# A macaron block with gated delta-rule attention on one core: beta in the decay exponent, T and softplus on the scalar engine, the output product on 32x32 tiles

## The reference

```
ffn(y):   xr, xk = mixes of y and of y one token earlier
          out = sigmoid(xr W_r) * ((relu(xk W_k)^2) W_v)
attn(y):  q, k, v = silu(conv4(y W))      q = q/|q| * 16^-0.5    k = k/|k|
          beta = sigmoid(y Wb)            g = -exp(A_log) * softplus(y Wa + dt_bias)
          per token and head:  S = S exp(g)
                               S = S + k outer ((v - k S) * beta)
                               o = q S
          out = (o * rsqrt(mean(o^2) + 1e-5) * norm_w * silu(y Wg)) Wo
x = x + 0.5 ffn(norm x);   x = x + attn(norm x);   x = x + 0.5 ffn(norm x)
```

## Time and profile before

| | before |
|---|---|
| runs | 1873.6, 1883.21, 1891.46 us |
| profiled execution, its own time | 1883.35 us |
| its span, first to last instruction | 1881.6 us |
| mean granted TensorE clock | 0.965 |
| busy: PE, PE weight loads, VectorE, ScalarE, GpSimd | 92%, 79%, 81%, 58%, 23% |
| MATMUL records on PE | 45,312 |

### The profile page before, as it was taken

One profiled execution on the slowest core, in us unless ns is written; L12 is line 12 of the kernel. 1 busy time (PEld: TensorE's weight loads), 2 busy tenths in 40 slices (PEclk: granted clock), 3 DMA queues, 4 the chain that ended last, 5 costly groups with the idle time before them and its releaser, 6 DMA issues.

```text
span 1881.6 us, 101829 instructions
## 1 busy us (share of the span) xinstructions
PE 1739.6 (92%) x45312; PEld 1486.7 (79%) x45312; DVE 1521.0 (81%) x4294; ACT 1089.1 (58%) x2002; POOL 438.4 (23%) x357
## 2 busy tenths in 40 slices
PE   5699999999999999999999999999999999999986
PEld 4587888787888788888888888888888878888775
DVE  4877889887888988888887888898788898887852
ACT  5556665555665565666565666555566555565533
POOL 0222221222221222222121222122222222222200
PEclk9889999999999999999999999999999999999877
DMA  3000000000000000000000000000000000000000
GB/s 113 2 3 4 15 14 4 15 14 15 15 15 9 9 15 15 15 15 15 3 15 14 15 15 15 9 9 14 15 15 15 9 9 9 9 9 10 9 9 13
DMA packets 21590, 26.50 MB, mean 14 GB/s; under 512 B 2209, under 2 KB 20769, under 8 KB 21153
## 3 DMA queue, kind: packets, MB, share of 16 engines
q1 hardware_dynamic: 21152, 19.99, 3.3%
HBM read 11.59 MB, written 8.39 MB: 11 GB/s over the span
## 4 chain that ended last, share of the span: by engine, by line
PE 53%; DVE 28%; issue 11%; ACT 1%; POOL 1%; DVEq 1%; ACTq 0%; POOLq 0%
PE ps L244 23%; PE ps L226 11%; PE ps L235 8%; DVE CV L1067 6%; DVE prod L1082 4%; DVE TZ L1083 3%; PE ps L219 2%; PE ps L400 2%; DVE T L1102 2%; PE ps L212 2%; DVE st L1035 2%; DVE XR L1056 1%; PE ps L357 1%; PE ps L461 1%; PE ps L372 1%
## 5 line engine op out<-in xcount | busy, mean ns | idle before, releaser
L1067 DVE SCALAR_TENSOR_TENSOR CV<-ps,cw,CV 128x256 f32<-128x256 f32 x576 | 250.8, 477 | 22.2 <-ACT CV L686 15.0
L244 PE MATMUL ps<-QE,S 64*64 64x16 f32 x4096 | 251.6, 209 | 2.0 <-ACT S L631 1.3
L244 PE MATMUL ps<-WP,V 64*64 64x16 f32 x4096 | 250.1, 208 | 0.0
L244 PEld LDWEIGHTS ps<-QE,S 64*64 64x64 f32 x4096 | 216.4, 138 | 35.0 <-issue 31.2
L244 PEld LDWEIGHTS ps<-WP,V 64*64 64x64 f32 x4096 | 217.4, 138 | 0.0
L244 PEld LDWEIGHTS ps<-WP,KD 64*64 64x64 f32 x4096 | 127.1, 137 | 36.5 <-DVE WP L1125 22.7
L1082 DVE TENSOR_TENSOR prod<-A,TZ 128x30 f32<-128x30 f32 (+7 forms) x480 | 139.0, 290 | 13.3
L967 POOL TENSOR_TENSOR OSQ<-OSQ,SQ 128x512 f32<-128x512 f32 x32 | 40.6, 1269 | 459.8 <-ACT OSQ L840 459.8
L244 PEld LDWEIGHTS ps<-SA,M 32*32 32x32 f32 x8192 | 91.0, 108 | 68.9 <-issue 34.3
L244 PE MATMUL ps<-SA,M 32*32 32x16 f32 x8192 | 117.9, 181 | 28.8 <-DVE SA L1096 18.4
L244 PE MATMUL ps<-KQI,K 64*64 64x48 f32 x4096 | 141.8, 221 | 1.4 <-DVE CV L1067 0.7
(11 more groups left out here) (152 smaller groups left out, 4055.4 us busy)
## 6 DMA issues: line engine op xcount, KB each, us to landing
X<-in_x SPq DMA_DIRECT2D x32, 256.0 KB, 2.9
out_x<-X SPq DMA_DIRECT2D x32, 256.0 KB, 2.3
KQI<-in_blocks SPq DMA_DIRECT2D x2, 256.0 KB, 4.2
w_r_ffn<-in_wT_r_ffn SPq DMA_DIRECT2D x1, 256.0 KB, 3.3
w_k_ffn<-in_wT_k_ffn SPq DMA_DIRECT2D x1, 256.0 KB, 3.5
w_v_ffn<-in_wT_v_ffn SPq DMA_DIRECT2D x1, 256.0 KB, 4.4
w_k<-in_wT_k SPq DMA_DIRECT2D x1, 256.0 KB, 4.3
w_q<-in_wT_q SPq DMA_DIRECT2D x1, 256.0 KB, 4.5
```

What stands on the lines that cost most here:

```text
L244: last = mm(ps[rows, o:o + n], stat[rows, pk].rearrange("p s c -> p (s c)"), mov[rows], **flags)
L1067: last = stt(d4[:, m], src, cw[:, i, m, tap:tap + 1], d4[:, m], ALU.mult, ALU.add)
```

## The change

It has five parts.

1. The output product on 32x32 tiles. S4 and V4 become S2 and V2 with 2 slots. Each pack now takes 4 + 4 matmuls on 4 tiles instead of 2 + 2 on 2 tiles; ScalarE fills each with 2 operations instead of 4. The product is cut into 8 segments instead of 4.
2. Beta in the decay exponent. Before, `beta_in` (4 matmuls of 128x128) added log(beta) to the decays and a second exponential gave EA; be and be2 scaled the output of `t_product`. Now GpSimd puts log(beta) on the diagonal of the step matrix ST (`beta_diag`, `stat1`), so that E has beta in it. `beta_in`, `exp_a`, `beta_log`, `b_diag` and `b_reduce` go.
3. T and softplus on ScalarE. `t_out0/1` move from VectorE (2 operations each) to ScalarE (3 each). ScalarE's softplus part has 5 small operations (L772 to L780, before 2); VectorE keeps 5, before 9.
4. Fewer, wider VectorE operations: KP and AT become one tile GK, M2 and QE one tile MQ, so a `gram` takes 3 operations instead of 4 and a `d_out` 1 instead of 2. MQ has two buffers.
5. Finer segments, another order on each engine and another table of PSUM banks. Solving is cut into 30 segments, each 1 operation; `conv` waits per tap instead of for all before it; `t_product` has 4 segments, `b_product` 4. `k_proj`, `q_proj` and `ffn1_r` run a step earlier, others move within the step.

The diff, cut to its core:

```
-        K4, KD4, V4, S4 = (sb(n, [P, PACKS, HT, C]) for n in ("K4", "KD4", "V4", "S4"))
+        K4, KD4 = (sb(n, [P, PACKS, HT, C]) for n in ("K4", "KD4"))
+        V2, S2 = (sb(n, [P, PACKS, 2, C]) for n in ("V2", "S2"))
...
-                for pk in range(h * PACKS // 4, (h + 1) * PACKS // 4):
+                for pk in range(h * PACKS // 8, (h + 1) * PACKS // 8):
                     o = PS["o"] * BANK + pk * C
-                    pairs(o, C, S4, pk, QE[g % 2][:, pk * C:(pk + 1) * C], start=True, stop=False)
-                    last = pairs(o, C, V4, pk, WP[g % 2][:, pk, U:], start=False, stop=True)
+                    pairs(o, C, S2, pk, MQ[g % 2][:, pk, U:], start=True, stop=False)
+                    last = pairs(o, C, V2, pk, WP[g % 2][:, pk, U:], start=False, stop=True)
...
-            def beta_in(g):
-                pe.wait_ge(s["lb"], g + 1)
-                pe.wait_ge(s["e"], g + 1)
-                for ub in range(M * B):
...
             def d_product0(g):
                 pe.wait_ge(s["wp"], 2 * g + 1)
                 pe.wait_ge(s["gram_used"], 4 * g + 4)
+                if g < GROUPS - 1:
+                    pe.wait_ge(s["cv"], 6 * g + 12)
+                    pe.wait_ge(s["tapv"], g + 2)
...
             def ffn1_r(g):
                 pe.wait_ge(s["xr1"], g + 1)
+                pe.wait_ge(s["relu1"], g + 1)
...
+            def t_out0(g):
+                act.wait_ge(s["t_ps"], 4 * g + 2)
...
+                for h in range(2):
+                    own.done(af(WP[g % 2][:, rows, h * C:(h + 1) * C], src[:, :, C:U], ACT.Copy, scale=slot[:, h:h + 1]))
+                nc.scalar.copy(WP[g % 2][:, rows, U:], src[:, :, 0:C]).then_inc(s["wp"], 1)
...
+            def beta_diag(g):
+                tt(packs(LD[:]), along(cz[:, BH:2 * BH]), over_packs(diag), ALU.mult).then_inc(s["ld"], 1)
...
-                own.done(tt(packs(QE[g % 2][:])[:, rows], packs(QP[:])[:, rows], src[:, :, U:], ALU.subtract))
-                tt(M2[:, rows].rearrange("p k s c -> p k (s c)"), GI2[:, rows], src[:, :, 0:U], ALU.subtract).then_inc(s["mt"], 1)
+                tt(MQ[g % 2][:, rows], GQ[:, rows], src, ALU.subtract).then_inc(s["mt"], 1)
```

More of the change, by code:

```diff
@@ new lines, in _ @@
+                on(ffn1_r, step)
+                on(turn3, step - 4)
+                on(o_product, step - 3, 4)
+                on(o_product, step - 3, 5)
+                on(ffn1_v, step)
+                on(k_squares, step - 1)
+                on(o_product, step - 3, 6)
+                on(o_product, step - 3, 7)
+                on(v_proj, step - 1)
+                on(t_product, step - 2, 0)
+                on(t_product, step - 2, 1)
+                on(decay_sums, step - 1)
+                on(ffn3_k, step - 4)
@@ new lines, in _ @@
+                on(t_product, step - 2, 2)
+                on(t_product, step - 2, 3)
+                on(o_squares, step - 3)
+                on(turn2, step)
+                on(d_product0, step - 2)
+                on(d_product1, step - 2)
+                on(d_product2, step - 2)
+                on(d_product3, step - 2)
+                on(b_product, step - 2, 0)
+                on(k_proj, step)
+                on(decay_steps, step - 1)
+                on(b_product, step - 2, 1)
+                on(q_proj, step)
@@ L618, in _ @@
+                on(b_product, step - 2, 2)
+                on(b_product, step - 2, 3)
+                on(ffn3_r, step - 4)
+                on(chain, step - 2, 0)
+                on(gram0, step - 1)
+                on(gram1, step - 1)
+                on(gram2, step - 1)
+                on(chain, step - 2, 1)
+                on(gram3, step - 1)
+                on(chain, step - 2, 2)
         @block.scalar
@@ L865, in rstd2 @@
                 root(1, s["rstd2"])
-            def soft_ln(g):
-                act.wait_ge(s["uz"], g + 1)
-                af(lu[:], uz[:], ACT.Ln).then_inc(s["lnu"], 1)
             def norm2(g):
@@ L927, in _ @@
+                on(tap_q, step - 1)
+                silu_set()
+                on(tanh3, step - 5)
+                on(xt1, step)
+                on(s_slots, step - 3)
+                ln_exp_set()
+                on(soft_exp, step - 1)
+                on(rstd3, step - 4)
+                silu_set()
+                on(silu_v, step - 2)
+                on(silu_k, step - 1)
+                on(relu1, step)
+                on(norm3, step - 4)
                 on(xt3, step - 4)
-                silu_set()
@@ L929, in _ @@
-                on(silu_k, step - 1)
-                on(tap_q, step - 1)
-                on(s_slots, step - 3)
+                on(silu_q, step - 1)
+                on(square_k, step - 1)
                 on(gate, step - 1)
-                on(relu3, step - 4)
-                on(relu1, step)
-                on(silu_q, step - 1)
-                on(tanh3, step - 4)
-                on(tap_v, step - 1)
+                on(tanh1, step)
+                ln_exp_set()
+                on(k_root, step - 1)
@@ L939, in _ @@
+                on(gates_wide, step - 1)
         @block.gpsimd
@@ new lines, in _ @@
+                on(gram1, step - 2)
+                on(chain, step - 3, 1)
+                on(gram2, step - 2)
+                on(gram3, step - 2)
+                on(chain, step - 3, 2)
+                on(a_turn, step - 2)
+                on(chain, step - 3, 3)
+                on(chain, step - 3, 4)
+                on(solve_mul, step - 2, 0)
+                on(solve_sub, step - 2, 0)
+                on(chain, step - 3, 5)
+                on(solve_mul, step - 2, 1)
+                on(chain, step - 3, 6)
```

745 lines of the change are left out of this document (333 added, 412 removed), and 6 rows, old and new, of the table names.

## The result

The changed kernel takes 1819.6 us in the median of 4 runs (1808.4 to 1826.6), the kernel before 1880.3 us beside it: a ratio of 0.967, 95% interval 0.960 to 0.974. It is 3.3% faster. Forecast were 1799 us in a range of 1740 to 1868. The profiled execution took 1821.5 us, its span is 1819.7 us.

What follows compares the result with a forecast made beforehand. PE, busy 92% of the span, was taken as the bound, nearly without gaps in steady state. The terms sum to -2.57 us a period, 84 us in all, so 1883 - 84 = 1799 us, range 1740 to 1868.

Steps and rivals of the forecast that it cites:

- the likeliest case: The prediction's own forecast for the whole kernel: 1799 us, within 1765 to 1835 us, chance 0.48.
- the part outside the periods: Filling and draining outside the 31 periods: 165.4 us before, 4.2 us less for the work of the 32nd group.
- Output product: PE's output product on 32x32 tiles: 512 MATMUL in 4.76 us instead of 7.88, -3.12 us a period.
- the row of a like shape: Profile row of 32x16 matmuls on 32x32 tiles: 9.3 ns each, taken to show that four tiles overlap the overhead.
- Beta: Beta's product leaves PE, and its replacement on GpSimd costs 0: -1.09 us a period.
- The wait for OT: PE's wait for OT at the output projection goes, since OT is there more than 10 us early: -0.86 us a period.
- Link gaps: Chain links 3 to 6 follow one another, so PE waits 1.4 us for copied state, before 0.52: +0.9 us a period.
- relu1: A new wait of PE's `ffn1_r` for relu1 on ScalarE, which reads the bank they share: +0.9 us a period.
- Supply: PE's instruction packets, 13.1 a period against 11.2: waits for issue 1.6 us in place of 1.18, +0.4 us a period.
- Tight places: Places where VectorE or ScalarE may be late, such as `d_product0` waiting for `conv_v`: +0.3 us a period.
- the supply as the bound: Rival: instruction packets come each 4.4 us and bind PE, period 57.6 us, 1952 us in all, chance 0.07.
- the rule that refilling stays hidden: The skill's rule that issue hides refilling of 256-instruction blocks: supply term -1.18 us a period, result 1750 us.

Runs made afterwards that it cites:

- experiment 1: The changed kernel with the output product back on 64x64 tiles (S and V in 4 slots), all else as changed: 1861.9 us, ratio 0.985 to the kernel before.
- Experiment 6: The changed kernel with the four 128x128 matmuls of decay_steps issued twice into the same place: 1816.5 us, ratio 0.964 to the kernel before.
- Experiment 3: The changed kernel with PE's order altered so fast 32x32 pieces stand one by one between larger products: 1845.1 us, ratio 0.974 to the kernel before.
- experiment 2: The kernel before with only the output product put on 32x32 tiles, in the old order with four pieces a step: 1934.2 us, ratio 1.023.
- Experiment 7: The changed kernel with the output product's eight pieces joined in four pairs, same matmuls and tiles: 1893.3 us, ratio 1.005 to the kernel before.
- experiment 4: The changed kernel with three stretches of small matmuls on constants (32x32, 64x64, 128x128 tiles) ahead of PE's first step: 2386.0 us in one run.
- experiment 8: The changed kernel with the output product's first half (S, MQ) on 64x64 tiles, the other on 32x32: 2133.2 us, ratio 1.134 to the kernel before.
- Experiment 9: The changed kernel with two 128x128 matmuls on constants after each of chain links 3, 4 and 5: 1817.9 us, ratio 0.963 to the kernel before.

## Why the prediction was right, and where it was not

The time came out 20.6 us above the forecast, within the likeliest case's own range. 31 x (53.26 - 52.8) = 14 us of it are the period, 7.5 us the part outside the periods, which I let shrink by 4.2 us and which grew by 3.3; the profiled execution lies 1.9 us above the median, which takes as much off. The terms:

- Output product, -3.12 us. The remainder gave 2.49 us in the old order and 2.76 in the new one. The tiles do overlap, as the row of a like shape said; a piece of the changed kernel that stands alone takes 0.66 us from start to start (row 1034.47 to `w_g` at 1035.13), two in a row 1.22, so the eight take some 5.0 us for 4.76. Right in kind, 0.2 us too large by these rows and 0.4 to 0.6 by the remainder, and only for PE's own work: with all that follows from them the tiles brought 1.43 us (experiment 1), where this term and that for supply make 2.72.

```profile
1034.47 0.25 PE L242 MATMUL ps<-MQ,S 32*32 32x16 f32 x8
...
1035.13 2.00 PE L462 MATMUL ps<-YT,w_g 128*128 128x256 f32 x8
```
- Beta, -1.09 us. Experiment 6 put most of that work back (0.89 us) at another place and the time stayed. As far as that run shows, this term is worth nothing in the changed kernel. That is the step which failed: "time taken from PE comes off the period as long as no new wait takes it". It supposed that the waits and the clock are independent of the work.
- The wait for OT, -0.86 us: right, it is gone.
- Link gaps, +0.9 us: +0.66 (36.5 against 16.2 us).
- relu1, +0.9 us: 0.03. PE came later than I had it, probably since it waits for issue and runs at the lower clock more. Experiment 3 shows how near the two paths lie: issue down by 0.97 us, relu1 up by 0.55.
- Supply, +0.4 us: +1.16. The count of packets was right and the spacing, 3.8 us by the earlier trace rows, was too (3.76 measured). I had compared them only over a period. What counts is the density within a stretch: experiments 2 and 7 have as many packets as the changed kernel (422 and 420) and wait 4.18 and 3.17 us a period for 2.38.
- Tight places, +0.3 us: under 0.1.
- No term at all for the clock: +0.74 us.

Together the three surplus terms (relu1, link gaps, tight places: 1.35 us) nearly paid for the two that were missing or small (clock and supply: 1.50 us), and 0.65 us were lacking in the work (0.3 came back from small waits of before, for XR above all, which had no term), of which finer pieces are the likely cause: 0.2 us show in the rows of the output product, and experiment 3 shows that more changes between large and small matmuls cost. So the time was right in part by luck. Experiment 1 says the same without the remainder: the tiles with supply were forecast at 2.72 us and brought 1.43, all else was forecast at -0.15 us and brought 0.67; 1.3 us too much and 0.8 too little nearly cancel.

Of the rivals, the supply as the bound (1952 us) had the right mechanism, and in the old order it decides the sign (experiment 2). What keeps it away here is in part the cutting into eighths, the part of the change that I had priced at nothing. Experiment 7 prices it at up to 2.4 us a period, its new wait for XT and the lower clock with it. It isn't all: the joined pieces wait 3.17 us for issue, the old order 4.18, and what else in the new order does it wasn't tested.

The Trainium skill, "Runtime: NRT & Kernel Launch", Instruction fetch mechanics, gave 1750 us in the prediction by the rule that refilling stays hidden. The runs are against it: 17.5 us of issue in experiment 1, 78 us in the changed kernel, 125 us at the head of the list in experiment 2, each time in stretches of small matmuls.

What stays open: how much of the falls of the clock comes from small matmuls and how much from standing still. That standing still isn't needed is shown: in experiment 4 the clock stayed at the lower level through 219 us of small matmuls without a gap, and experiment 8 had few waits and the lowest clock. Experiment 9 changed both at once, so what each gives in the links isn't known. And the 3.3 us outside the periods weren't looked into.

## What to carry to other kernels

Where one engine is the bound by its busy share, weigh its work in three parts: work at the full clock, waits, and time at the lower clock. A cut in work that thins the engine out can be taken back by the other two, so test by putting work back, which cost nothing here. On this kernel small matmuls paid where they were cut into short stretches (3.3% faster) and not where they stood in longer ones (experiments 2 and 7); and where PE must wait briefly again and again ahead of a large product, one matmul on constants in the gap can be worth its place (1.3% here).

## What the runs showed that I had not expected

- A packet of 256 instructions mostly takes 3.45 to 4.0 us to come, 3.76 in the mean, when PE uses them as fast as it can (experiment 4, at the lower clock; 3.84 in the median at the upper, experiment 2); in experiment 4 PE then mostly stands still for 1.55 to 2.1 us.
- Small matmuls that keep PE busy without a gap for 219 us leave the clock at the lower level (experiment 4).
- Changing tile size at every call of `pairs` costs 80 to 110 ns a change and the clock with it (experiment 8, 13% slower than before), though neither tile size alone does that.
- The granted clock often falls for 3.4 us at the end of a stretch of links with waits of 0.36 us between them (11 of 21 falls); with two fillers in each gap no fall began there, and `wo` went from 81.9 to 63.8 us.
- The faster tiles alone made the old kernel 2.3% slower (experiment 2).
